# Moving one edge list's indirect sends on GpSimd from four early stages of a graph network to three later ones

## The reference, cut to what matters

```python
# the first layer: a convolution over src -> dst, with edge_index
x = x + _L0_gnn_ref(_layernorm(x, axis=-1), ..., edge_index)
# attention with its own edge list, then a mixture of 4 experts
x = x + _L0_ffn_ref(_layernorm(x, axis=-1)[None], ..., L0_ffn_edge_index)[0]
# typed attention over src -> dst: a softmax per destination, then weighted sums
x = x + _L1_gnn_ref(_layernorm(x, axis=-1), ..., node_type_4, edge_type_8, src, dst)
# a mixture of 8 experts (every node passes all of them)
x = x + _L1_ffn_ref(_layernorm(x, axis=-1)[None], ...)[0]
...
# the last graph layer: z[edge_row] += edge_weight * h[edge_col], edge_row = src, edge_col = dst
msg = edge_weight[:, None] * h[edge_col]
z = jax.ops.segment_sum(msg, edge_row, num_segments=n_nodes)
```

## Time and profile before

| what | value |
| --- | --- |
| median of 3 runs | 6601.27 us (6598.57, 6604.53, 6601.27) |
| span of the profiled execution | 6235.3 us |
| its own time | not given apart from its span; against the median, 366 us lie around the span |
| busy, of the span | PE 4642.0 us (74%), DVE 3534.9 us (57%), POOL 2468.4 us (40%), ACT 1673.7 us (27%) |
| counting block | about 531 to 915 us from the span's start |
| the two convolution blocks | about 931 to 1107 us, 1108 to 1209 us |
| first mixture | about 1834 to 2195 us |
| `hgt_w_`, `hgt_a_` | about 3120 to 3231 us, 3231 to 3487 us |
| next mixture | about 3657 to 4195 us |

### The profile page before, as it was taken

The page is one execution under the profiler, slowest core; times in us unless marked ns, Lnnn a source line. Parts: engine busy times, 40 slices in busy tenths (PEclk is TensorE's granted clock), DMA queues, the critical chain, the costliest instruction groups (busy, mean ns, idle before and its releaser), DMA issues. The chain is left out here.

```text
span 6235.3 us, 89789 instructions
## 1 busy us (share of the span) xinstructions
PE 4642.0 (74%) x23352; PEld 3272.4 (52%) x23409; DVE 3534.9 (57%) x7052; ACT 1673.7 (27%) x3879; POOL 2468.4 (40%) x2746
## 2 busy tenths in 40 slices
PE   5876878755459977666569889999999495465558
PEld 2213435544347733445446667777777363355546
DVE  8988983656673354999848634441111333555544
ACT  0954643411112233111100233332222121200022
POOL 0857966557528733777400000001111201377700
PEclk8998999855559988788769989999999598676779
DMA  0002438412110068999847210003333331233300
GB/s 30 2 11 98 167 140 258 153 31 35 41 55 15 1 216 316 337 320 324 229 162 236 81 23 10 10 28 131 100 102 99 92 98 58 65 102 103 99 20 21
DMA packets 401474, 688.78 MB, mean 110 GB/s; under 512 B 116811, under 2 KB 286930, under 8 KB 396650
## 3 DMA queue, kind: packets, MB, share of 16 engines
q1 hardware_dynamic: 302786, 430.80, 21.5%
q0 software_dynamic: 98304, 255.53, 13.3%
q10 hardware_dynamic: 192, 0.15, 0.0%
HBM read 453.27 MB, written 233.01 MB: 110 GB/s over the span
## 5 line engine op out<-in xcount | busy, mean ns | idle before, releaser
L3325 POOL CAST sagel_piece<-x 128x1600 fp32r<-128x1600 f16 (+1 forms) x75 | 112.3, 1498 | 1608.0 <-DMA x<-counts 1165.0
L517 POOL DMA_INDIRECT back_sorted<-back_space x391 | 412.3, 1055 | 239.1 <-POOLq L1713 170.0
L1027 POOL DMA_INDIRECT wsum_a_rows<-table,edge_src x416 | 414.6, 997 | 225.3 <-issue 119.1
L2127 POOL DMA_INDIRECT big<-hgt_table,edge_key x448 | 423.6, 945 | 199.1 <-issue 139.7
L1041 PE MATMUL wsum_a_ps<-wsum_a_hot,wsum_a_rows 128*128 128x128 f32 x1664 | 320.7, 371 | 238.0 <-DMA wsum_a_rows<-table,edge_src 142.4
L1041 PEld LDWEIGHTS wsum_a_ps<-wsum_a_hot,wsum_a_rows 128*128 128x128 f32 x1664 | 294.7, 274 | 264.1 <-DVE big L1068 183.8
L517 POOL DMA_INDIRECT own_sorted<-big x256 | 289.7, 1132 | 291.6 <-issue 290.7
L3381 PE MATMUL sagel_ps<-sagel_piece,sagel_high 128*128 128x512 f32 (+1 forms) x1050 | 400.3, 389 | 0.8 <-issue 0.8
L2175 PE MATMUL hgt_s_pq<-big 128*128 x1344 | 246.0, 347 | 188.7 <-DVE hgt_s_tmp L2214 155.1
L3381 PE MATMUL sagel_ps<-sagel_piece,sagel_low 128*128 128x512 f32 (+1 forms) x1050 | 380.8, 376 | 0.0
L722 PE MATMUL cnt_ps<-cnt_hot_s,cnt_hot_d 128*128 128x512 bf16 (+1 forms) x1736 | 311.7, 333 | 79.7 <-DVE cnt_hot_s L704 73.0
(11 more groups left out here) (968 smaller groups left out, 10862.5 us busy)
## 6 DMA issues: line engine op xcount, KB each, us to landing
hgt_edge_values<-big SPq DMA_DIRECT2D x112, 512.0 KB
big<-hgt_edge_values SPq DMA_DIRECT2D x112, 512.0 KB, 3.7
x<-counts SPq DMA_DIRECT2D x75, 400.0 KB, 3.1
x<-counts SPq DMA_DIRECT2D x75, 384.0 KB, 3.0
counts<-big SPq DMA_DIRECT2D x25, 832.0 KB
counts<-big SPq DMA_DIRECT2D x25, 768.0 KB
big<-counts SPq DMA_DIRECT2D x30, 640.0 KB
counts_turned<-big SPq DMA_DIRECT2D x30, 640.0 KB, 3.8
```

Of the source, the lines that this page charges most:

```text
L517: self.nc.gpsimd.indirect_dma_start(self.e.dram, bass.IndirectOffsetOnAxis(ap=self.adr[:, c:c + 1], axis=0), self.rec[:, c, :], None).then ...
L1027: nc.gpsimd.indirect_dma_start(rows[n % DEEP][:, u, :], None, table, bass.IndirectOffsetOnAxis(ap=e.src[:, g:g + 1], axis=0)).then_inc(gat ...
L2127: nc.gpsimd.indirect_dma_start(rows[n % DEEP][:, u, :], None, at.table, bass.IndirectOffsetOnAxis(ap=at.index[:, g:g + 1], axis=0)).then_i ...
```

## The change

All 391 sends of `back` are taken out of the counting, the two convolution blocks and the first mixture, and put beside three later blocks: 60 sends beside `hgt_w_`, 150 beside `hgt_a_`, 181 beside the next mixture. The counting keeps its 98 sends of `own`, the first mixture keeps `order.write`. The records, their addresses and the spare tile have to live longer, so `back_space` and a `back_pace` tile are allocated further out; to make room, the typed attention's `scores` move from a tile of their own into the end of the buffer `big4`. No computation is added or removed.

```diff
@@ program
             bufs = [pair.enter_context(nc.sbuf_tensor(n, [P, NT * D], F32)) for n in ("big1", "big2")] + [big3, big4]
+            n_all = -(-A["src"].shape[0] // P) * 5
+            back_space = pair.enter_context(nc.sbuf_tensor("back_space", [P, n_all], F32))
+            back_pace = {"back": pair.enter_context(nc.sbuf_tensor("back_pace", [P, PACE], F32))[:]}
...
-                n_all = -(-A["src"].shape[0] // P) * 5
-                back_space = c.enter_context(nc.sbuf_tensor("back_space", [P, n_all], F32))
-                pace = {n: c.enter_context(nc.sbuf_tensor(f"{n}_pace", [P, PACE], F32))[:] for n in ("own", "back")}
+                pace = {"own": c.enter_context(nc.sbuf_tensor("own_pace", [P, PACE], F32))[:]}
...
-                    def rest(pool):
-                        own_sort.send(pool, 158, own_sort.C, pace)
-                        back_sort.send(pool, 0, 100, pace)
-                    build_counts(nc, kit, edges, counts, counts16, bufs, rest)
+                    build_counts(nc, kit, edges, counts, counts16, bufs, paced(158, own_sort.C, own_sort))
                     scale_and_heavy_nodes(nc, kit, g)
-                    gcn_stage(nc, kit, g, x, bufs, counts, counts16, counts_t, paced(100, 160, back_sort),
-                              paced(160, 205, back_sort))
+                    gcn_stage(nc, kit, g, x, bufs, counts, counts16, counts_t)
                     own_sort.fetch()
                 order.find(A["node_type_4"], c)
-                def send_and_order(pool):
-                    back_sort.send(pool, 205, back_sort.C, pace)
-                    order.write(pool)
-                gat_moe_stage(nc, kit, A, x, bufs, own, send_and_order)
-            hgt_stage(nc, kit, A, x, bufs, edges, order)
-            soft_moe_stage(nc, kit, A, x, bufs, rdeg_dram)
+                gat_moe_stage(nc, kit, A, x, bufs, own, order.write)
+            back_part = lambda lo, hi: lambda pool: back_sort.send(pool, lo, hi, back_pace)
+            hgt_stage(nc, kit, A, x, bufs, edges, order, back_part(0, 60), back_part(60, 210))
+            soft_moe_stage(nc, kit, A, x, bufs, rdeg_dram, back_part(210, back_sort.C))
@@ hgt_stage
-        scores, top, top3 = sb("scores", [P, groups, H]), sb("top", [P, NT, H]), sb("top3", [P, NT, 3, H], BF16)
+        top, top3 = sb("top", [P, NT, H]), sb("top3", [P, NT, 3, H], BF16)
+        scores = b4[:, NT * D - groups * H:].rearrange("p (g h) -> p g h", g=groups)
+        assert groups * H <= NT * D // 2
...
-            edge_weights(nc, kit, "hgt_w", at, scores, top3)
+            edge_weights(nc, kit, "hgt_w", at, scores, top3, beside1)
...
-            edge_sums(nc, kit, "hgt_a", at, scores, acc[:])
+            edge_sums(nc, kit, "hgt_a", at, scores, acc[:], beside2)
@@ edge_weights, and the same in edge_sums
         with nc.Block() as block:
+            block.gpsimd(beside)
+
             @block.sync
@@ soft_moe_stage
-                    of("L1_ffn_Wo"), bo, gates, x, stats=kit.stats)
+                    of("L1_ffn_Wo"), bo, gates, x, beside=beside, stats=kit.stats)
@@ gcn_stage
                     put_spare(pool)
-                    beside1(pool)
...
-                    beside2(pool)
```

More of the change, by code:

```diff
@@ L1285, in gcn_first, with gcn_stage @@
     return g
-def gcn_stage(nc, kit, g, x, bufs, counts, counts16, counts_t, beside1, beside2):
+def gcn_stage(nc, kit, g, x, bufs, counts, counts16, counts_t):
     big1, big2, big3, big4 = bufs
@@ L1873, in columns, with soft_moe_stage @@
     return ap2d.rearrange("e (k p) -> p (e k)", p=P)
-def soft_moe_stage(nc, kit, A, x, bufs, rdeg_dram):
+def soft_moe_stage(nc, kit, A, x, bufs, rdeg_dram, beside):
     b2 = bufs[1]
@@ L2286, in _, with edge_weights @@
                 split3(nc, link, [top3[:, :, k, :] for k in range(3)], top, rest[:])
-def edge_weights(nc, kit, nm, at, scores, top3):
+def edge_weights(nc, kit, nm, at, scores, top3, beside):
     e, H = at.edges, at.heads
@@ L2491, in _, with edge_sums @@
                 act.wait_ge(raised, batches)
-def edge_sums(nc, kit, nm, at, weights, acc):
+def edge_sums(nc, kit, nm, at, weights, acc, beside):
     e, H, dv = at.edges, at.heads, at.dv
@@ L2710, in gat_moe_stage, with hgt_stage @@
                     stats=kit.stats)
-def hgt_stage(nc, kit, A, x, bufs, e, order):
+def hgt_stage(nc, kit, A, x, bufs, e, order, beside1, beside2):
     b1, b2, b3, b4 = bufs
```

## The result

The changed kernel takes **6651.02 us** (median of 6651.49, 6650.56, 6653.11 and 6650.23) against 6601.41 us for the kernel before in the same series: ratio 1.0078, 95% interval 1.0064 to 1.0093, so 42 to 61 us slower. The forecast was 6633 with a range of 6595 to 6650. The direction was right, the size was not: +50 us instead of +32. One execution of this kernel, in a later series, took 13144 us, twice the time of all the others, and is left out of every comparison.

The account below looks back on a forecast made before the run. POOL was taken to end no block before; DVE limits the counting, PE the convolution and first mixture. Terms -19 + 0 + 0 + 1 + 50 + 0 = +32 us on the median of 6601.27 gave 6633, range 6595 to 6650.

Parts of the forecast that it names:

- the counting, -19 us: Counting: with 100 sends of `back` gone, DVE's L704 speeds up and the block shortens by 19 us, of a possible 12 to 22.
- Rival D: Counting gains nothing because PE or ACT takes over as its limit at once: +51, 6652 us; chance 0.05.
- `hgt_a_`, +50: `hgt_a_`: sends fall into step with DVE's two-input multiply, one per 2.24 us; the other 34 form a tail, +50 us.
- Rival A: `hgt_a_`: sends stay free, not held by the multiply, and end before the block does; -18, 6583 us; chance 0.12.
- Rival B: `hgt_a_`: no locking in step, sends wait as random ones would, 1.86 us a round: +23 there, 6606 us; chance 0.12.
- Rival C: `hgt_a_`: each send, once first, also holds DVE for 0.85 us; steps grow by some 0.5 us, 6689 us; chance 0.03.
- `hgt_w_`, +1: `hgt_w_`: 60 rounds take about 96 of 111 us, DVE's one-hots may be stretched: +1 us, bounds 0 and +4.
- Next mixture: 0: Next mixture: 181 rounds at 1.56 are 282 us under 534, so no change.
- Convolution: 0: Convolution: PE is the cover at the same pace with or without sends: 0 us, bounds 0 and -2.
- First mixture, 0 within -1 and 0: First mixture: 186 rounds go, but POOL had ended before DVE and PE sets the pace: 0 us, bounds 0 and -1.

## Why the prediction was right and wrong

**The failed step is the counting, -19 us.** The text said "In the counting DVE is the limit: busy 174.4 of 182 us" and took 0.75 us for an L704 from a window of 16. The runs show -0.4 (378.4 to 378.0 us), less than the 1.5 by which kernels with the same loop differ, and no change (1.0003) for the kernel in which only these sends were moved. Both halves of the reading were wrong. A busy share of 96% did not make DVE the limit: the rounds of PE's loop last as long without the sends as with them, 6.75 us on average for eight groups (378/56), of which 6.42 are PE's own matmuls and pauses, and pauses do not show as busy; a share says nothing of who waits. And the 12 us window caught DVE while it ran ahead into its four buffers. These rows of the kernel before span that window:

```profile
893.63 2.63 DVE L704 TENSOR_SCALAR cnt_hot_s<-cnt_iota,cnt_source 128x1600 bf16<-128x1600 int16 x4
894.82 2.88 PE L722 MATMUL cnt_ps<-cnt_hot_s,cnt_hot_d 128*128 128x512 bf16 x16 [0.17 <-issue]
...
905.68 2.67 DVE L704 TENSOR_SCALAR cnt_hot_s<-cnt_iota,cnt_source 128x1600 bf16<-128x1600 int16 x4
907.66 2.88 PE L722 MATMUL cnt_ps<-cnt_hot_s,cnt_hot_d 128*128 128x512 bf16 x16 [0.17 <-issue]
```

From the first to the last are four batches; DVE took (905.68 - 893.63)/4 = 3.01 us each, the 0.75 of the prediction times four, but PE took (907.66 - 894.82)/4 = 3.21: DVE's lead grew from 1.2 to 2.0 us, and the counting went at PE's pace. "PE is already busy 10.2 of 12 us" stood in the text as a doubt, and it was the right one. Rival D (the counting gains nothing, 6652) was right in kind, and had 0.05 because of that window. That its 6652 lies 1 us from the 6651 measured is partly luck: the block terms below add up to 58 us, not 51.

**`hgt_a_`, +50: right in kind and nearly in size, +54.6.** 116 sends before the end of the last multiply (116 forecast), 34 behind it at 1.52 us, DVE's L2541 and L2547 no longer than before (median 0.693 and 1.218 us), the block's end 311 us after its start (290 to 310 forecast). The missing 4.6 us are POOL's exit. The text put "a memset that is not" held down to the earlier trace rows, where the memset starts 0.85 us after L557 has ended and shows nothing; the run with two memsets does. Rival A falls with every run with sends there. Rival B falls with the two memsets; without any it gave the better time, since three sends in two steps are near what a random wait would give. Rival C falls for these kernels, since steps last 2.24 us in both; without the memset steps did grow, by 0.12 us. What stands against my account in detail is the moment that counts, the send's start and not 0.13 us later; with one memset both give one send per step.

The rows of this block bear on both rules of the Trainium skill (SBUF — State Buffer). In the shortened multiply's run most of the holding goes away with the long two-input multiply, and what is left starts inside the one-hot, which has two SBUF inputs as well; this fits the rule in "Who interferes with whom". The inference in the same list, that descriptor generation needs only the write interface, would have left the sends at 0.98 us, and they took 1.64. The exclusive lock of "SBUF: two separate sides" would also hold DVE up behind a send that started first; at 3603.86 one did, by 0.03 us, and the multiply took 1.23 us instead of 1.22. In the 29 cases of this run in which a send started at most 0.13 us before the multiply, the multiply took 1.21 to 1.25 us, so for these two instructions the measurement speaks against that half of the rule.

**`hgt_w_`, +1: 0.** 111.3 us both times, the sends took 98.6 us (96 forecast). **Next mixture: 0,** as forecast, 181 rounds at 1.56. **Convolution: 0,** as forecast: its first block varies between 171 and 180 us over all profiles whether or not sends run beside it, its second lasts 104.6 to 105.0. **First mixture, 0 within -1 and 0: +3.** The text said that the type order comes earlier and counted only POOL's end; it did not ask what its first DMA would meet there. The +3 is the mean over the kernels with the writing in front; the changed kernel's own two profiles have waits of 7.9 and 9.3 us, 1.7 and 3.1 more than the 6.2.

Sum of what was measured: 0 + 3 + 0 + 54.6 = 58 us, inside the intervals of both comparisons (42 to 61, 46 to 63), if above their middles. One sum of the prediction does not come out: the bounds that it lists for its terms, the convolution's and the mixture's with them, give 6620 to 6647, not 6618 to 6645; 6651 lies above either.

## What to carry to other kernels

Before work is taken off an engine, look for the one that the others wait for by its rhythm (first to last instruction, divided by the rounds of its loop) with and without the work; a busy share near 100% can belong to an engine that is just as fast as the real limit, and a few microseconds of a window behind a ring of buffers show its filling. Indirect sends, spaced out by a memset and placed beside a loop whose DVE instruction reads two SBUF operands for half of the step, ran in step with it here, so count rounds, not microseconds: 116 sends were free and 150 cost 54 us. And when something is taken from the front of a queue, ask what now stands first, and beside whose loads.

## What the runs showed that I had not expected

- A send that starts 0.01 us before a two-input multiply takes 0.97 us, one that starts inside it ends 0.84 to 0.87 us after it; the shorter one-hot, with two SBUF operands, does the same. (Sends that start in the last 0.1 us of either take their own 0.97 us.)
- PE's loop with numbers fetched per batch costs 0.17 us between batches and 0.49 us at its end; eight batches a round instead of two saved 11 to 12 of 378 us.
- Without its memset a send beside `hgt_a_` keeps pace with the block, but the block grows from 256.7 to 268.3 us, and only while the sends run.
- The changed kernel's 4.6 us between POOL's last instruction and the next block shrink to at most 2.3 when POOL ends with the others.
